# Layer 1's mixture of experts in a graph network: rows gathered through an inverse list, results scattered by token, normalisation joined to the combination

## The reference, cut to what matters

```python
h = layer_norm(x)                                   # 3125 x 256, becomes XN
p = h @ gate_w + gate_b                             # 3125 x 16
weight, expert = top_2(p), softmaxed over the two
y[n, k] = relu(h[n] @ w1[expert[n, k]] + b1[...]) @ w2[expert[n, k]] + b2[...]
m = h + weight[n, 0] * y[n, 0] + weight[n, 1] * y[n, 1]
x = x + layer_norm(m) * gamma + beta
```

## Time and profile before

| | us |
|---|---|
| median of three runs | 4360.08 |
| lowest and highest | 4359.11, 4368.43 |
| the profiled execution | 4384.73 |
| its span, first to last instruction | 4383.0 |
| mean granted clock of TensorE in it | 0.848 |

### The profile page before, as it was taken

How to read it: one execution, slowest core, us unless ns; L and a number is a source line. 1 busy time by engine, 2 the same in 40 slices (tenths; PEclk the granted TensorE clock), 3 DMA queues, 4 the chain that set the end, 5 groups by cost and what they waited for, 6 DMA issues and landing times. The chain is left out here.

```text
span 4383.0 us, 52512 instructions
## 1 busy us (share of the span) xinstructions
PE 3195.9 (73%) x17915; PEld 2449.1 (56%) x17916; DVE 1390.7 (32%) x3307; ACT 804.2 (18%) x2090; POOL 2275.9 (52%) x1830
## 2 busy tenths in 40 slices
PE   0999955574999993596089999968697555553993
PEld 0555543454999993596078878855443333332562
DVE  3333355442441114011621111133432434442005
ACT  0666622211000001232121100023200000001220
POOL 5587777775666666765236656600002666662003
PEclk9999977777999995798599999969897666665996
DMA  8663222228999886699133333300143333332222
GB/s 338 233 191 84 4 6 6 11 8 246 276 286 276 253 233 156 156 245 228 42 127 133 134 119 131 107 15 0 39 140 123 91 91 92 93 90 75 98 90 69
DMA packets 368093, 562.71 MB, mean 128 GB/s; under 512 B 177053, under 2 KB 246493, under 8 KB 351584
## 3 DMA queue, kind: packets, MB, share of 16 engines
q1 hardware_dynamic: 201740, 393.74, 28.0%
q0 software_dynamic: 158320, 122.06, 15.2%
q10 hardware_dynamic: 7824, 44.20, 2.5%
HBM read 413.40 MB, written 145.88 MB: 128 GB/s over the span
## 5 line engine op out<-in xcount | busy, mean ns | idle before, releaser
L455 POOL DMA_INDIRECT count_cells<-cells_count,added_row x391 | 645.4, 1651 | 282.8 <-issue 119.4
L874 POOL DMA_INDIRECT weight_cells<-added_weight,added_row x391 | 610.2, 1561 | 321.2 <-DMA weight_cells<-added_weight,added_row 181.4
L915 POOL DMA_INDIRECT g3g_got<-relations,g3g_idx x416 | 405.1, 974 | 685.7 <-ACTq L86 498.2
L1429 PE MATMUL g_acc<-XN,g_blocks 125*125 125x128 f32 x5000 | 567.8, 275 | 55.0 <-DMA g_blocks<-count_cells 52.6
L1429 PEld LDWEIGHTS g_acc<-XN,g_blocks 125*125 125x125 f32 x5000 | 559.6, 189 | 59.6 <-issue 52.8
L1742 PE MATMUL g_acc<-g_H,g_blocks 125*125 125x256 f32 x2500 | 557.6, 382 | 23.8 <-DMA g_blocks<-weight_cells 13.2
L1659 POOL DMA_INDIRECT slots_dram<-sort_rec,sort_row x392 | 379.8, 969 | 349.0 <-issue 112.5
L928 PE MATMUL g3g_pp<-g3g_got,g3g_hot 128*125 128x256 f32 x832 | 341.7, 560 | 271.4 <-issue 205.8
L1742 PEld LDWEIGHTS g_acc<-g_H,g_blocks 125*125 125x125 f32 x2500 | 471.4, 189 | 102.5 <-issue 31.8
L928 PEld LDWEIGHTS g3g_pp<-g3g_got,g3g_hot 128*125 128x125 f32 x832 | 203.8, 270 | 409.5 <-issue 247.8
L954 DVE TENSOR_TENSOR X<-X,g3g_pp 125x256 f32 x416 | 175.5, 422 | 349.2 <-DMA edges_other<-digits_dram 183.7
(11 more groups left out here) (624 smaller groups left out, 4530.4 us busy)
## 6 DMA issues: line engine op xcount, KB each, us to landing
g_blocks<-count_cells SPq DMA_DIRECT2D x500, 312.5 KB
g_blocks<-weight_cells SPq DMA_DIRECT2D x50, 1562.5 KB
count_cells<-edges_stripe ACTq DMA_DIRECT2D x25, 1562.5 KB
weight_cells<-edges_stripe POOLq DMA_DIRECT2D x25, 1562.5 KB
f1e_w<-in_L_ffn_w SPq DMA_DIRECT2D x68, 512.0 KB
relations<-g_ys SPq DMA_DIRECT2D x25, 896.0 KB
f_w<-in_L_ffn_w SPq DMA_DIRECT2D x16, 1024.0 KB, 9.9
bins<-zeros SPq DMA_DIRECT2D x1, 8704.0 KB, 32.8
```

The lines of the kernel that those rows point to most:

```text
L455: pool.indirect_dma_start(out=rows, out_offset=bass.IndirectOffsetOnAxis(ap=g.cell_row[:, t:t + 1], axis=0), in_=g.cell_count[:, t:t + 1], ...
L874: pool.indirect_dma_start(out=rows, out_offset=bass.IndirectOffsetOnAxis(ap=g.cell_row[:, t:t + 1], axis=0), in_=g.cell_weight[:, t:t + 1] ...
L915: pool.indirect_dma_start(out=got[:, j, :], out_offset=None, in_=table[:, :], in_offset=bass.IndirectOffsetOnAxis(ap=idx[:, n:n + 1], axis ...
L1429: last = nc.tensor.matmul(acc[0:P, i % ACCS, 0:128], blocks[0:P, i % BLOCKS, t * P:(t + 1) * P], rhs[p][:, t, :], start=(t == 0), stop=(t ...
```

## The change

The rows are no longer put in order by scattering them. The sort's positions are turned into their inverse on TensorE: DVE writes one-hot matrices of the place within a tile (`slot`) and of the tile (`tile`, times the number of the pair plus one), and 50 matrix products add up to a 128 x 64 table that says for each place which pair stands there. From it come two lists of whole numbers: `node` (the row of `table256`, 0 for empty places) and `to` (the row of the new array `moe`, one for each pair in the order of the nodes, with rows of their own for empty places).

In the expert stage POOL gathers the rows of each tile from `table256` by `node` and scatters the results of each tile to `moe` by `to`; SP does neither any more. Into each of the 64 steps goes one of the transfers that add weights; 39 remain behind the stage. The results then come back by ten plain loads. `ys` has four places instead of two, the working buffers have rooms of their own, and `XN` stays where it is. The combination, the norm (its statistics taken group by group, its 25 tiles all on ACT), `gamma` and the addition to `X` make one stage instead of three. The copy to `table256` is issued right after the gate. DVE's and POOL's lists for the expert stage are written out; SP, PE and ACT keep their loops. A wait for `g.cleared` moves to the last layer, and `results` shrinks.

```diff
@@ class Norm
-    def start_dve(self, dve):
+    def start_dve(self, dve, taken=False):
         nc, st, mean, spread, var = self.nc, self.st, self.mean, self.spread, self.var
-        for t in range(T):
-            nc.vector.bn_stats(st[0:P, t, :], self.src[0:P, t, :])
-        dve.drain()
+        if not taken:
+            for t in range(T):
+                nc.vector.bn_stats(st[0:P, t, :], self.src[0:P, t, :])
+            dve.drain()
@@ layer1_ffn, the list
+            @block.vector
+            def _(dve):
+                n = 2 * T // CUT
+                nc.vector.tensor_scalar(high[0:P], posf[0:P], 1.0 / 128, -63.5 / 128, ALU.mult, ALU.add)
...
+                nc.vector.tensor_tensor(tile[0:P], wide(g.iota[0:P, 0:SLOTS], P, 2 * T, SLOTS), deep(high[0:P], P, 2 * T, SLOTS),
+                                        ALU.is_equal)
+                dve.drain()
+                nc.vector.tensor_tensor(tile[0:P], tile[0:P], deep(value[0:P], P, 2 * T, SLOTS), ALU.mult)
+                for c in range(CUT):
+                    nc.vector.tensor_tensor(slot[0:P, c], wide(g.iota[0:P, 0:128], P, n, 128),
+                                            deep(posf[0:P, c * n:(c + 1) * n], P, n, 128), ALU.is_equal)
+                    dve.drain().then_inc(slots_hot, 1)
...
+                dve.wait_ge(listed, 1)
+                nc.vector.tensor_copy(found[:, :], inverse[:, 0:SLOTS])
...
+            @block.tensor
+            def _(pe):
+                for c in range(CUT):
+                    pe.wait_ge(slots_hot, c + 1)
+                    for m in range(2 * T // CUT):
+                        k = c * (2 * T // CUT) + m
+                        last = nc.tensor.matmul(inverse[:, 0:SLOTS], slot[0:P, c, m, :], tile[0:P, k, :],
+                                                start=(k == 0), stop=(k == 2 * T - 1))
+                last.then_inc(listed, 1)
...
-            @block.gpsimd
-            def _(pool):
-                pool.wait_ge(g.cleared, 16)
-                pool.wait_ge(placed, 1)
-                for t in range(T):
-                    for k in range(2):
-                        pool.indirect_dma_start(out=g.bins[:, :],
...
-            add_weights(nc, g, EARLY_WINDOWS, NW)
@@ layer1_ffn, the expert stage
+            add_weights(nc, g, 0, EARLY_WINDOWS)
+
+            @block.gpsimd
+            def _(pool):
...
+                pool.wait_ge(g.phase_done, listed)
+                for n in range(AHEAD):
+                    gather(n)
+                for n in range(SLOTS):
+                    pool.wait_ge(x_turned, n + 1)
+                    gather(n + AHEAD)
+                    pool.wait_ge(y_put, n + 3)
+                    pool.indirect_dma_start(out=g.moe[:, :], out_offset=bass.IndirectOffsetOnAxis(ap=to[:, n:n + 1], axis=0),
+                                            in_=ys[:, n % AHEAD, :], in_offset=None).then_inc(stored[n % AHEAD], 16)
+                    t = EARLY_WINDOWS * WT + n
+                    if t % WT == 0:
+                        pool.wait_ge(g.weights_added, 16 * t)
+                    pool.indirect_dma_start(out=rows, out_offset=bass.IndirectOffsetOnAxis(ap=g.cell_row[:, t:t + 1], axis=0),
...
+            add_weights(nc, g, EARLY_WINDOWS + SLOTS // WT, NW)
...
-                        sp.wait_ge(x_turned, n + 1)
-                        load_rows(n + AHEAD, j)
...
-                        sp.dma_start(results[bass.ds(n, 1)].rearrange("a p d -> (a p) d"), ys[:, j % 2, :]).then_inc(stored[j % 2], 16)
@@ layer1_ffn, the combination
+                    for c in range(C):
+                        for lo, hi in STRIPS:
+                            sp.dma_start(Y[lo:hi, c * G:(c + 1) * G], moe[lo:hi, c * G:(c + 1) * G]).then_inc(back[c], 16)
...
+                        for t in range(c * G, (c + 1) * G):
+                            nc.vector.bn_stats(norm.st[0:P, t, :], g.XN[0:P, t, :])
                     dve.drain()
+                    norm.start_dve(dve, taken=True)
+                    for c in range(C):
+                        tiles = slice(c * G, (c + 1) * G)
+                        dve.wait_ge(norm.by_act, (c + 1) * G)
+                        nc.vector.tensor_tensor(g.XN[0:P, tiles], g.XN[0:P, tiles], wide(gamma[0:P, :], P, G, D), ALU.mult)
+                        dve.drain()
+                        nc.vector.tensor_tensor(g.X[0:P, tiles], g.X[0:P, tiles], g.XN[0:P, tiles], ALU.add)
```

More of the change, by code:

```diff
@@ L2054, in layer1_ffn @@
-            stored = [sem1(f"stored{j}") for j in range(2)]
+            xs, ys = sb1("xs", [128, AHEAD, D]), sb1("ys", [128, AHEAD, D])
+            xT, hT = sb1("xT", [128, 2, D]), sb1("hT", [128, 2, F])
+            pT, pH, pY = (ps1(m, [128, 2, 512]) for m in ("pT", "pH", "pY"))
+            b_loaded, w1_loaded = ([sem1(f"{m}{j}") for j in range(AHEAD)] for m in ("b_loaded", "w1_loaded"))
+            x_loaded, stored = g.moved[0:AHEAD], g.moved[AHEAD:2 * AHEAD]
+            loads, stores = 16 * (SLOTS // AHEAD + 1), 16 * (SLOTS // AHEAD)
@@ L2078, in _ @@
                     load_bias(e[j], j)
-                sp.wait_ge(scattered, done)
-                for j in range(AHEAD):
-                    load_rows(j, j)
                 with sp.Fori(0, BODIES) as i:
@@ L2093, in _ @@
                         sp.wait_ge(y_put, n + 3)
[L2094 removed]
                         load_bias(e[j], j)
[L2097 to L2098 removed]
                 for j in range(AHEAD):
[L2100 removed]
+                    sp.wait_ge(stored[j], stored_before[j] + stores)
+                    sp.wait_ge(x_loaded[j], x_before[j] + loads)
                     sp.wait_ge(b_loaded[j], 16 * (BODIES + 1))
@@ L2167, in _ @@
                 dve.sem_inc(y_put, 2)
-                with dve.Fori(0, BODIES) as i:
+                for i in range(BODIES):
                     for j in range(AHEAD):
@@ L2216, in _ @@
                             dve.drain()
-            layer_norm(nc, g, "f1m", g.XN, Y[0])
-            with stage(nc, g) as block:
-                @block.vector
-                def _(dve):
-                    nc.vector.tensor_tensor(Y[0][0:P], Y[0][0:P], wide(gamma[0:P, :], P, T, D), ALU.mult)
-                    dve.drain()
-                    nc.vector.tensor_tensor(g.X[0:P], g.X[0:P], Y[0][0:P], ALU.add)
+                        for t in range(c * G, (c + 1) * G):
+                            nc.vector.bn_stats(norm.st[0:P, t, :], g.XN[0:P, t, :])
+                    dve.drain()
+                    norm.start_dve(dve, taken=True)
[3 more added lines that the diff above has]
+                        nc.vector.tensor_tensor(g.XN[0:P, tiles], g.XN[0:P, tiles], wide(gamma[0:P, :], P, G, D), ALU.mult)
+                        dve.drain()
+                        nc.vector.tensor_tensor(g.X[0:P, tiles], g.X[0:P, tiles], g.XN[0:P, tiles], ALU.add)
+                @block.scalar
+                def _(act):
+                    norm.start_act(act)
+                    for t in range(T):
+                        norm.tile_act(t)
 def layer2_ffn(nc, g, a):
```

117 lines of the change are left out of this document (60 added, 57 removed).

## The result

| us | before | after |
|---|---|---|
| median of six runs | 4359.6 | 4385.2 |
| lowest and highest | 4353.5, 4370.3 | 4375.6, 4397.4 |
| ratio, 95% interval | | 1.0058 (1.0036 to 1.0079) |
| the profiled execution | 4384.7 | 4397.4 |

The change makes the kernel 25.6 us slower; 4373 was forecast, in a range from 4345 to 4408. The profiled executions differ by 12.7 us only, almost exactly the +12.5 of the prediction.

A forecast was written before the change was run, and what follows sets the result against it. PE set the expert stage's pace at 3.74 us a tile; POOL would become the pace at 4.40. Parts of -30.3, +52.4 and -9.6 sum to +12.5 us on 4360.1, giving 4373, range 4345 to 4408.

The forecast's parts named there:

- the pace: Expert stage: POOL's gather, scatter, add and gaps take 4.40 us a tile against PE's 3.74, making the stage +52.4 us.
- The rival of late landings: Expert stage: gathers land too late; at 11 us from issue the step is 4.95, total 4407; chance 0.17.
- The clock: Expert stage: with PE 83% busy it could fall to 0.93, making PE's tile 4.0 us, still under POOL's.
- the list: After the sort: PE begins after 9.7 us and makes 100 passes in 21.2 us at clock 0.50.
- ACT's 13.8 us: Before ACT's first ReLU: idle time assumed to remain, within 20.5 us kept from PE's first work to first result.
- part one: Sort to first result: PE starts 37.5 us after the sort instead of 67.8, -30.3 us; bounds -42 to -23.
- The first rival: Before the first result: ACT's idle time vanishes and PE's clock rises, 23 us earlier, total 4350; chance 0.14.
- Its sign: The first rival decides if the first result comes under 45 us after the sort.
- part three: Last result to layer 2's norm: POOL's remaining adds set the end, 104.3 us against 113.9, -9.6; bounds -23 to +4.
- four waits, two like those beside heavy loads (4.3): Behind the expert stage: POOL's window waits, two of 4.3 us and two of 1.8, together 12.2 us.
- lower bounds, -42 + 42 - 23: Fastest case of the three parts' bounds; all bounds together were given as 4339 to 4413.
- The third rival: DVE doesn't hold POOL up, as adds might read their lists ahead: +2, 4362, no difference; chance 0.13.

The follow-up runs named there:

- second pair: Later profiles of the kernel before and the changed kernel, both unchanged, each on its own chip: 4279.1 and 4314.2 us.
- moved_adds: Changed kernel with 17 adds moved from behind the expert stage, 12 ahead of the first gather and 5 behind the fifth: 4282.2 us, ratio 1.0004.
- early38: Changed kernel with two more windows (16 adds) ahead of the first gather, 23 instead of 39 left behind the expert stage: 4285.8 us, ratio 1.0015.
- after: The changed kernel's first profile, nothing further altered: median 4385.2 us, profiled execution 4397.4 us.
- control_after: The changed kernel, unchanged, run again on another chip for a second profile: 4314.2 us, ratio 1.0078.
- loads_one_by_one: Changed kernel, but SP loads a group of `moe` only when the group before has landed: 4304.0 us, ratio 1.0062.
- three_stages: Changed kernel, but the norm and the gamma multiplication with the addition to X are stages of their own again: 4313.7 us.
- adds_behind: Changed kernel with all 103 late adds behind the expert stage, none beside the experts: 4490.9 us, ratio 1.024.
- no_late_adds: Changed kernel without the 103 adds behind the early windows, so layer 2's edge weights are incomplete: 4211.4 us, 0.9833 of the kernel before.

## Why the prediction was right, and where it was off

**Right: the pace.** "4.40 us, more than PE's 3.74" became 4.51 and some waits, and +52.4 became +52.8 (+54.4 in the second pair). The three transfers together were 0.10 us dearer beside one another than in the rows taken, 6 us over the stage, and the waits for windows cheaper: five with 5.5 us beyond their gaps, instead of seven with 10.3. The two errors nearly cancel. Leaving the adds out brought PE's 3.74 back, which shows the cause. The rival of late landings, which needed 11 us from issue to landing, is wrong: 5.2 without the adds, 4.0 in `moved_adds`. The clock, which the text let fall to 0.93 in a bound, stayed at 0.99.

**Right: the list.** PE started 38.0 us after the sort instead of 37.5, 100 passes took 21.6 instead of 21.2 us, at clock 0.50 ahead of them and during them.

**Wrong in what it took from one row: ACT's 13.8 us.** The text kept 20.5 us from PE's first work to the first result and said of ACT's idle time "and it still does". It was a stop of one execution. With it gone on both sides the gain of part one is 76.3 - 50.8 = 25.5 us in the second pair, and 27 against the changed kernel's first profile, not 30.3. It also explains why the profiled pair agreed with +12.5 while the medians are 25.6 apart: the before profile alone held 12 us that the usual execution doesn't have. The first rival, which lets the stall go in the changed kernel only, was right about that stall and mistaken about the kernel it was compared with. Its sign, a first result under 45 us after the sort, didn't come (49.3), since PE's clock didn't rise during the list.

**Wrong by 13 to 16 us: part three.** Forecast -9.6, measured +3.6 in the first pair and +6.5 in the second, over its upper bound of +4. By the terms of the sum, counted from the last scatter's start (104.3 forecast, 115.5 measured):

| us | forecast | measured |
|---|---|---|
| scatter and the last add of the stage | 2.9 | 2.9 |
| 39 adds and what DVE holds them up by, 34 gaps | 81.5 | 79.8 |
| five waits for windows | 16.5 | 21.6 |
| landing of the last | 1.8 | 3.8 |
| POOL's drain | none | 6.0 |
| the block's end | 1.7 | 1.3 |

The step "four waits, two like those beside heavy loads (4.3)" took its price from the expert stage before, where adds waited beside its loads; behind 6.4 MB issued at once it was 14.8, and with one group in flight 4.64. And the drain had no term at all: it stood in no view of busy time and was hidden under DVE before. "But the next block begins only when POOL has come to the meeting" was right and names the reason why all of the joined norm (+0.4 us when undone) brought nothing.

**The sum, and luck.** Both misses push the same way: in an execution without the stop the stretch is 29 to 35 us longer, not 12.5, and the medians say 25.6 and, on the second chip, 33.9. The direction, the pace and POOL's part in the block's end were understood. That the profiled pair met +12.5 was luck. A slip in the text: its lower bounds, -42 + 42 - 23, make 4337 and not 4339; nothing hangs on it.

**DVE against POOL.** One add of 6.54 us under `beta` was forecast as "about 7", and came. The three late adds of up to 2.67 us, and the four beside DVE's products in `early38`, say the same for operations of 1.5 and 3.5 us. The third rival is out. What the Trainium skill (SBUF — State Buffer, Who interferes with whom) infers, that a `tensor_tensor` leaves the making of descriptors alone since that needs only the write side, doesn't hold for these transfers, while its neighbouring rule, that two inputs on chip contend with GpSimd's reads, agrees with all of these rows. The measurement decides. The combination (`scalar_tensor_tensor`, two inputs on chip, 0.42 us each) made an add 1.67 to 1.85 us long instead of 1.55.

**The conclusion.** Adds, gathers and scatters together fill POOL's list from the early windows to the block's end. The change took 50 scatters off the head of that list, a gap of 31.7 us came in their place, and 50 gathers at its tail gave way to 64 gathers and 64 scatters in the middle and 39 adds behind them. That PE had room beside them doesn't count: POOL was the longer of the two.

## What to carry to other kernels

Add up the list of an engine that issues indirect transfers over the whole span between the points where it can be idle, not stage by stage: here 1.9 us an add, 1.3 a gather or scatter, and moving 17 of them into its idle time was worth 32 us, all that the change had cost there (33.9) but 2. Look at what an engine does after its last counted instruction; a drain of 6 us that another engine's work covered becomes the end of the block when the cover goes. And take a second profile of the kernel before when one idle time in it has no cause in the rows: 12 us of "before" were one execution's.

## What was not expected of the hardware

- POOL's drain behind indirect transfers takes time even when all of them have landed: 5.85 us in four profiles (`after`, `control_after`, `loads_one_by_one`, `three_stages`), 6.3 to 6.7 in three (`adds_behind`, `early38`, `moved_adds`), 19 to 26 us when it starts under a run of them, and 4.8 us when it starts under the last one (`no_late_adds`).
- A window of adds of 128 single values each (0.5 KB) kept POOL waiting for 12.6 to 18.8 us while 6.4 MB of loads issued at once were in flight (seven profiles), 11.0 with 2.6 MB, 4.6 and 6.9 with 1.3 MB, and 1.6 to 2.0 with none.
- POOL's transfers cost a little more where kinds alternate: an add 1.61 us between gathers and scatters, 1.54 alone beside the experts' loads; a gather 1.01 with the adds, 0.97 without.
